# Relative attention on one core: each head's scores from its own 32 rows of the array, two heads into two banks, and the causal mask of the turned scores made by a select on GpSimd

## The reference

```python
xn = _layernorm(x, axis=-1)
Qh, Kh, Vh = heads of xn @ W_q + b_q, xn @ W_k + b_k, xn @ W_v + b_v
idx = clip(k - q, -2, 2) + 2
scores = einsum('bhqd,bhkd->bhqk', Qh, Kh)
scores = (scores + einsum('bhqd,qkd->bhqk', Qh, rel_k_table[idx])) / scale
scores = where(causal, scores, -1e9)
attn = softmax(scores)
out = einsum('bhqk,bhkd->bhqd', attn, Vh) + einsum('bhqk,qkd->bhqd', attn, rel_v_table[idx])
return out @ W_o + b_o
```

## Time and profile before

| | |
|---|---|
| median of 3 runs | 3927.83 us (3923.24 to 3929.47) |
| the profiled execution: its time, its span | 3928.65 us, 3926.6 us |
| mean granted TensorE clock over the span | 0.986 |
| relative attention, first to last instruction | from the start to about 564 us |
| one sequence (four groups) in it | 63.63 us |
| busy share of the span: TensorE, VectorE, ScalarE, GpSimd | 94%, 78%, 58%, 66% |

### The profile page before, as it was taken

One profiled execution on the slowest core, in us unless ns is written; L12 is line 12 of the kernel. 1 busy time (PEld: TensorE's weight loads), 2 busy tenths in 40 slices (PEclk: granted clock), 3 DMA queues, 4 the chain that ended last, 5 costly groups with the idle time before them and its releaser, 6 DMA issues.

```text
span 3926.6 us, 163773 instructions
## 1 busy us (share of the span) xinstructions
PE 3690.6 (94%) x67712; PEld 2844.7 (72%) x67712; DVE 3058.0 (78%) x5829; ACT 2270.7 (58%) x4270; POOL 2597.4 (66%) x3029
## 2 busy tenths in 40 slices
PE   5999979999999999999999999999999999999998
PEld 3555557777767777677877678787677876777876
DVE  7666658888778888788887788887788887888876
ACT  3555546666546666456666366665466664566653
POOL 4545538787547887367887288775477873687870
PEclk8999989999999999999999999999999999999999
DMA  1000002222212222122222122222122221222220
GB/s 44 4 6 4 6 28 68 56 60 60 58 32 59 59 57 59 41 49 60 61 57 56 30 65 57 59 61 58 32 60 58 59 56 41 54 57 58 60 52 22
DMA packets 136313, 189.08 MB, mean 48 GB/s; under 512 B 38006, under 2 KB 58484, under 8 KB 135412
## 3 DMA queue, kind: packets, MB, share of 16 engines
q1 hardware_dynamic: 135540, 178.23, 17.7%
HBM read 22.67 MB, written 2.10 MB: 6 GB/s over the span
## 4 chain that ended last, share of the span: by engine, by line
PE 76%; issue 4%; DVE 2%; POOL 2%; ACT 0%; DMA 0%; POOLq 0%; SPq 0%; DVEq 0%; ACTq 0%
PE PS L1270 18%; PE PS L1417 10%; PE PS L1256 10%; PE PS L1294 8%; PE PS L1280 8%; PE PS L1258 8%; PE PS L1257 8%; PE PS L1476 2%; PE PS L1411 2%; PE PS L1454 1%; PE PS L1447 1%; POOL t L1182 1%; PE PS L1442 1%; POOL t L1187 0%; DVE m L1800 0%
## 5 line engine op out<-in xcount | busy, mean ns | idle before, releaser
L1182 POOL TENSOR_TENSOR t<-t 128x1024 f32<-128x1024 f32 x384 | 908.0, 2370 | 363.9 <-DVE t L1762 362.6
L1187 POOL TENSOR_TENSOR t<-t,rn 128x1024 f32<-128x1024 f32 x384 | 723.6, 1905 | 29.8 <-POOL rn L150 27.3
L1542 ACT ACTIVATE va<-PS 128x512 f32<-128x512 f32 x384 | 229.8, 599 | 614.4 <-PE PS L1258 611.6
L1760 DVE TENSOR_TENSOR t<-PS,rope 128x512 f32<-128x512 f32 x768 | 523.2, 681 | 26.1 <-ACT sq L1577 24.5
L1256 PE MATMUL PS<-w_hi,xh 128*128 128x512 f32 x1152 | 514.2, 446 | 22.3 <-DVE xl L1063 11.3
L1577 ACT ACTIVATE sq<-PS 128x512 f32<-128x512 f32 x768 | 454.1, 593 | 33.0 <-PE PS L1258 17.7
L1270 PE MATMUL PS<-constants,t 128*128 128x128 f32 x3072 | 443.8, 277 | 19.8 <-POOL t L1187 12.8
L1258 PE MATMUL PS<-w_lo,xh 128*128 128x512 f32 x1152 | 458.5, 398 | 0.0
L1257 PE MATMUL PS<-w_hi,xl 128*128 128x512 f32 x1152 | 457.5, 397 | 0.0
L1767 DVE TENSOR_REDUCE ss<-sq 128x16 f32<-128x1024 f32 x384 | 448.3, 1209 | 0.0
L1270 PEld LDWEIGHTS PS<-constants,t 128*128 128x128 f32 x3072 | 351.9, 141 | 68.9 <-POOL t L1187 15.9
(11 more groups left out here) (168 smaller groups left out, 7869.8 us busy)
## 6 DMA issues: line engine op xcount, KB each, us to landing
vs<-va SPq DMA_DIRECT2D x768, 130.0 KB
vs<-va SPq DMA_DIRECT2D x768, 65.0 KB
t<-in_L_ffn_Wqkv SPq DMA_DIRECT2D x18, 512.0 KB, 4.4
w_out<-in_L_ffn_Wo SPq DMA_DIRECT2D x6, 512.0 KB, 3.9
a_normed<-in_L_attn_x SPq DMA_DIRECT2D x8, 256.0 KB, 7.0
a_xo<-in_L_attn_x SPq DMA_DIRECT2D x8, 256.0 KB, 2.8
out<-total SPq DMA_DIRECT2D x8, 256.0 KB, 3.5
w_raw<-in_L_ffn_W SPq DMA_DIRECT2D x6, 341.0 KB
```

The lines of the kernel that those rows point to most:

```text
L1182: pool.tensor_tensor(mine[:, i, :], mine[:, i, :], t2[:, i, :], ALU.add).then_inc(done, 1)
L1187: pool.tensor_tensor(h, h, bc(rn[:, H * i:H * (i + 1)], 2, HB), ALU.mult).then_inc(done, 1)
L1760: dve.tensor_tensor(o1, src, bc(rope[:, 2 * i, t, :], 1, 8), ALU.mult)
```

## The change

Four things change, all in `relative_attention`.

- `kT` has one tensor per group in place of four: no zeros, no copies. `join_keys` is one instruction on 128 rows, where it was four of 32 rows. The zero fill at the start goes.
- A score product takes only the 32 rows of its head. The two heads of a piece follow one another directly, on different rows of the array and into different banks.
- The last piece (j = 4), which held four heads in 256 columns each, becomes two pieces of two heads (j = 4 and 5), each 256 columns in each of two banks. `PIECES` is 6.
- The turned scores have no mask ahead of them. Instead, `close_future` on GpSimd writes zero over the future keys in `probs` after the exponentials, one select for each piece. `values` waits for it (`opened`) and no longer for ScalarE. `values(y, 0)` moves behind j = 3, and `values(y, 2)` behind the first turned piece of the next group. `weights` waits for the values of the group before piece by piece.

```diff
-        PIECES = 5
+        PIECES = 6
-        JOINS = 1 + G
+        JOINS = 2
-        kT = sb("a_kT", [P, NG, G, N], F32R)
+        kT = sb("a_kT", [P, NG, N], F32R)
...
             def join_keys(y):
                 wait_used(pool, ("proj", y, 1))
-                for r in range(G):
-                    rows = slice(32 * r, 32 * (r + 1))
-                    pool.wait_ge(joined, JOINS * y + 1 + r)
-                    pool.tensor_tensor(kT[rows, y % NG, r, 1:N], high[rows, 1, 0:N - 1].bitcast(F32), lowT[rows, 1, 0:N - 1],
-                                       ALU.add).then_inc(joined, 1)
-                pool.wait_ge(joined, JOINS * (y + 1))
+                pool.tensor_tensor(kT[:, y % NG, 1:N], high[:, 1, 0:N - 1].bitcast(F32), lowT[:, 1, 0:N - 1],
+                                   ALU.add).then_inc(joined, 1)
+
+            def close_future(y, j):
+                wait_used(pool, ("turn", y, j))
+                at, n = ((0, 1), (4 * P, 2), (8 * P, 1))[j // 2]
+                now = heads_of(j, at, n * P).rearrange("p g (n c) -> p g n c", n=n)
+                pool.affine_select(now, now, [[0, 2], [0, n], [1, P]], ALU.is_gt, 0.0, base=0, channel_multiplier=-1).then_inc(opened, 1)
...
             for y in range(GROUPS):
                 s, p = divmod(y, NG)
+                for j in range(3):
+                    close_future(y, j)
+                if y + 3 < GROUPS:
+                    join_queries(y + 3)
+                for j in range(3, PIECES):
+                    close_future(y, j)
...
-                q = lambda t: qT[:, g, P * t:P * (t + 1)]
-                k = lambda r, n: kT[:, g, r, 0:P * n]
+                blocks = (((3, 0, 4),), ((2, 0, 3), (0, 3, 1)), ((1, 0, 2),))[j // 2]
                 for a in range(2):
...
+                    at, n = ((3, 1), (2, 2), (1, 1))[j // 2]
+                    shut(tiles_of(bank(me, a), at, n), far_mask)
+                for t, at, n in blocks:
+                    for a in range(2):
+                        rows = head(j, a)
+                        done = score(bank(me, a)[:, P * at:P * (at + n)], qT[rows, g, P * t:P * (t + 1)], kT[rows, g, 0:P * n])
...
+                for t, at in (((0, 0),), ((3, 0), (1, 1)), ((2, 0),))[j // 2]:
+                    for a in range(2):
+                        rows = head(j, a)
+                        done = pe.matmul(bank(me, a)[:, P * at:P * (at - t) + N], kT[rows, g, P * t:P * (t + 1)],
+                                         qm[rows, y % 2, P * t:N], start=True, stop=True, skip_group_check=True)
...
-                for j in ((0, 1), (2, 3), (4,), ())[kt]:
-                    wait_used(pe, ("turn", y, j))
+                pe.wait_ge(opened, PIECES * y + (2, 4, 6, 4)[kt])
...
-                if y and j == 0:
-                    act.wait_ge(val_mm, 4 * y)
+                if y:
+                    act.wait_ge(val_mm, 4 * (y - 1) + (1, 3, 4)[j // 2])
...
-            dve.memset(kT[:].rearrange("p n g c -> p (n g c)").bitcast(F32), 0.0).then_inc(filled_in, 1)
             norm(0, TPS, 0)
```

More of the change, by code:

```diff
@@ L52 @@
 C_FAR = C_MQ0 + 2 * W
-C_FART = C_FAR + P
-C_SEL = C_FART + P
+C_SEL = C_FAR + P
 C_NEAR = C_SEL + P
@@ L365, in per_tile_head, with heads_of @@
             return h.rearrange("p t (h d) -> p t h d", h=H)
-        def of_heads(b, n):
-            return b[:, 0:G * n].rearrange("p (g c) -> p g c", g=G)
+        def heads_of(j, at, n):
+            return probs[:, 2 * (j % 2):2 * (j % 2) + 2, at:at + n]
         @block.sync
@@ L538, in turned @@
                 wait_slot(pe, me)
-                k = lambda r, t: kT[:, g, r, P * t:P * (t + 1)]
-                q = lambda t: qm[:, y % 2, P * t:N]
-                for a in range(2):
-                    b, r = bank(me, a), 2 * (j % 2) + a
-                    if j < 2:
-                        shut(b[:, 0:P], far_mask_t)
-                        done = score(b[:, 0:4 * P], k(r, 0), q(0))
-                    elif j < 4:
-                        shut(tiles_of(b, 0, 2), far_mask_t)
-                        score(b[:, 0:P], k(r, 3), q(3))
-                        done = score(b[:, P:4 * P], k(r, 1), q(1))
-                    else:
-                        shut(every_second(b, 0), far_mask_t)
-                        for h in range(2):
-                            done = score(b[:, 2 * P * h:2 * P * (h + 1)], k(2 * a + h, 2), q(2))
+                for t, at in (((0, 0),), ((3, 0), (1, 1)), ((2, 0),))[j // 2]:
[3 more added lines that the diff above has]
+                                         qm[rows, y % 2, P * t:N], start=True, stop=True, skip_group_check=True)
                 done.then_inc(filled(me), 1)
@@ L629, in _ @@
                     turned(y, j)
+                    if j == 0 and y:
+                        values(y - 1, 2)
                     if j == 0 and p == 1 and s + 1 < B:
@@ L637, in _ @@
                             turn_sums(s - 1, 3)
+                    if j == 3:
                         values(y, 0)
@@ L652, in _ @@
                 values(y, 3)
-                values(y, 2)
+            values(GROUPS - 1, 2)
             for i in range(TPS):
@@ L756, in maximum @@
                 else:
-                    target, source = maxima[:, y % 2, :, 5], bank(me).rearrange("p a (h c) -> p (a h) c", h=2)
+                    target, source = pair[:, :, 5], bank(me)[:, :, 0:2 * P]
                 dve.tensor_reduce(target, source, X, ALU.max).then_inc(used(me), 1)
@@ L841, in _ @@
             dve.wait_ge(const_in, 16)
+            dve.tensor_copy(kT[:, :, 0], rank["const"][:, C_SHUT:C_SHUT + 1].broadcast_to([P, NG])).then_inc(filled_in, 1)
             dve.wait_ge(filled_in, 2)
-            for r in range(G):
-                rows = slice(32 * r, 32 * (r + 1))
-                dve.tensor_copy(kT[rows, :, r, 0], rank["const"][rows, C_SHUT:C_SHUT + 1].broadcast_to([32, NG])).then_inc(filled_in, 1)
-            dve.wait_ge(filled_in, 2 + G)
             dve.wait_ge(bias_made, 10)
```

37 lines of the change are left out of this document (9 added, 28 removed).

## The result

| | before | after |
|---|---|---|
| median of the runs | 3925.53 us (4 runs, 3922.84 to 3929.47) | 3993.78 us (4 runs, 3984.91 to 3995.63) |
| the profiled execution's span | 3926.6 us | 3993.4 us |
| last copy of the sums begins | 551.42 us | 602.74 us |
| span behind it, the windowed layers above all | 3375.2 us | 3390.7 us |
| mean granted clock | 0.986 | 0.955 |

The ratio is 1.0164 (1.0152 to 1.0177): **slower by 1.6%**, where 3867 us and "faster" were predicted. The stage is 51 us longer, not 62 us shorter (54 and 8), and the windowed layers, which keep every instruction, take 15.5 us more.

What follows compares the result with a forecast made beforehand. TensorE's stream was taken to bound the relative attention stage. The sum was 3928.65 - 54 (groups) - 8 (start) + 1 (end) = 3867.7, given as 3867 us because the profiled execution is 0.8 above the median; range 3836 to 3905.

Steps and rivals of the forecast that it cites:

- 54 and 8: Relative attention: 54 us saved by 1.7 us net in each of 32 groups, 8 us by the earlier start.
- Prices of the pieces: TensorE's score pieces: 0.89 us for j = 0, 1; 1.11 for j = 2, 3; 0.67 for j = 4, 5.
- Rival 1: TensorE's score pieces: weight loads or shape changes cost the gain, 3905 or 3887 us; chance 0.24, including no overlap.
- Selects: GpSimd's selects over future keys: 3.5 us per group, bounds 2.8 and 5.1, so its load is no matter.
- the 1.5 us at which cover would be gone: GpSimd: at 1.5 us per select, the work covering both moved value products' waits for selects would no longer suffice.
- rival 3: Slow selects make GpSimd bound the relative attention stage: 4017 us at 7 ns per element; chance 0.07.
- Start: Start of the kernel: 5 us gained without the zero fill, 3 more from fewer key joins beside VectorE's norm.
- At granted clock 1.00: Relative attention stage: TensorE's clock read as 1.00 in the earlier profile, with prices and sum built on it.
- The last sentence of the prediction: Signs against it: select over 1.5 us, pairs 0.2 us apart, or stage clock leaving 1.00 because of 32-row strips.
- 0.3 us per group: Part of TensorE's 2.0 us saving per group lost to growing waits on VectorE's maxima, leaving 1.7 us net.
- the 3.8 us "that are there": TensorE's existing waits for VectorE's maxima per sequence, 1.29 us direct and 2.5 in held-back loads, expected to grow.
- The layers "unchanged": Windowed layers behind relative attention: every instruction is kept, so their time was counted unchanged.

Runs made afterwards that it cites:

- e4: Kernel before the change with one line moved: VectorE's zero fill of the keys behind the first norm instead of ahead of it; ratio to before 1.0009.
- e13: Kernel of e9 with four more 512-column mask products ahead of the second and third turned piece of each first group; ratio to before 1.0154.
- e5: Kernel before with selects for turned masks and moved value products; five pieces, all rows, zero fill behind the first norm; ratio to before 1.0023.
- e1: Changed kernel with score products on all 128 rows again (four padded key tensors, four joins, fill behind the norm); ratio to before 1.0045.
- e2: As e1, but natural score products on 32-row strips and only the turned ones on all rows; ratio to before 1.0154.
- e3: Changed kernel with 64-row strips in place of 32, two key tensors holding two heads each; ratio to before 1.0053.
- e12: Kernel before with GpSimd's near products moved into the fourth group and VectorE's sums over them behind the fourth maxima; ratio to before 1.0047.
- e9: Changed kernel with six 512-column mask products laid into TensorE's wait for the turned queries in every fourth group; ratio to before 1.0118.
- e7: Changed kernel with the masks on turned scores put back as products on all 128 rows, selects kept; ratio to before 1.0333.
- e15: Changed kernel with the previous group's last value products set ahead of the first turned piece instead of behind it; ratio to before 1.0224.
- e10: Changed kernel with GpSimd's near products moved into the fourth group and VectorE's sums over them behind the fourth maxima; ratio to before 1.0147.
- e14: Kernel of e5 with VectorE's zero fill of the keys ahead of the first norm, as in the kernel before; ratio to before 1.0028.

## Why the prediction was wrong

- **Prices of the pieces: right.** 0.88 for 0.89 us, 1.08 for 1.11, 0.68 and 0.63 for 0.67; no load or change of shape cost more. Rival 1 was not it.
- **Selects: right,** 2.97 us per group between the bounds, and rival 3 has no part. No select comes near the 1.5 us at which cover would be gone.
- **Start: near in the sum,** 9.5 us earlier for 8. How the fill (5) and the joins (3) share it isn't shown: e4, which only moves the fill, gains 3.1 us at the same place.
- **"At granted clock 1.00": this step failed, and it is the largest error.** The sum took the clock of the earlier trace rows for granted. The last sentence of the prediction named this way to fall, but it had neither a chance nor a price there; the 0.07 for "slower" was all for slow selects. In the changed kernel the third and fourth stretch ran at 0.61 and 0.68. At 1.00 the third stretch is 13.2 us (e13) and the fourth 18.05 less the filler's eight products of 0.21 us, thus 16.3, so a sequence would be 13.85 + 18.82 + 13.2 + 16.3 = 62.2 us (an estimate put together from two kernels). It is 71.7: **9.5 us a sequence, some 76 us in eight**, is the clock.
- **"0.3 us per group" taken back: this term failed too.** By the same estimate a sequence at full clock gains 63.6 - 62.2 = 1.4 us, which is 0.4 per group and not 1.7. TensorE's busy time did fall, by 1.81 us in the first stretch and 1.11 in the second, but it went into waits. The prediction looked for them at the maxima and shared them evenly. They came at the near terms, at the queries and at the sums, which it had called TensorE's time to catch up. Its starting point was too high as well: the 3.8 us "that are there" add a wait of the weight loads (2.1 us) to the wait of the product behind it (1.29), which is the same one, and TensorE idles 63.63 - 60.88 = 2.75 us in all. Some 5.4 us a sequence, 43 us in eight.
- The two make 119 us; the last copy is at 602.7 where the prediction has 551.4 - 62 = 489, 113 us off. With the 15.5 us of the layers that is the whole miss of 127 us, within 2.
- **The layers "unchanged":** their instructions are, their time is not. 15.5 us more here, and from 3374 to 3407 us over the kernels, in part by the clock (e5) and in part by idle time.

That the strips bring the clock down here is shown, by e1 and e2. What the clock asks for can be told only in part. Strips lower it (e1, e2, e3). So do longer waits on full rows (e12, and one sequence before). Work laid into a wait brings part of it back (e9), and work laid elsewhere doesn't (e7). All of this fits one account: the changed kernel does its work in less of TensorE's time and array, and stretches with little of both are followed by the lower level, at which projections take 2.08 us for 1.02. e15 and the spread within e13 do not follow from it, so the account is supported, not settled. The Trainium skill's page "TensorE: Matmul & The Clock Gate", section "HAM oscillation — how this bites in real kernels", tells of a kernel whose waits for DMA make the clock swing between its levels; the stretches at 0.61 and 1.00 within one sequence agree with it in kind, while the waits here are for VectorE.

For VectorE's differences the Trainium skill has a rule: its page "SBUF — State Buffer", section "SBUF: two separate sides", has a VectorE instruction with two SBUF inputs and a GpSimd instruction that reads SBUF exclude one another, for the whole of whichever starts first. 2.41 us for two differences beside the near products, and 0.24 us for one on average without them (e10), agree.

## What to carry to other kernels

A cheaper form of the bounding engine's work is worth its price only if the engine's clock and its partners keep up: read the granted clock by stretch, and ask of each saved microsecond which wait it turns into. A change that makes TensorE do more in less time should carry a rival "the clock falls", priced from rows: here the stretches it touches cost 9.5 us more. Take compound changes apart: up to the last copy of the sums, selects in place of masks on full rows won 16 us, the sixth piece alone lost 9.5 (both with the fill behind the norm, which alone won 3.7 in e4), both together lost 5 (e1), and the strips, added last, lost 46; one measurement of them all shows none of it. None of the fifteen is faster than the old program, for even the best stage lost its gain behind it.

## What was not expected of the hardware

- Masks laid into a wait of 1.38 us made a program 0.5% faster than without them (ratios 1.0118 and 1.0164, 14.7 us of it in the stage); smaller masks in every turned piece made it 1.7% slower (1.0333).
- The same instructions took 63.9 us (clock 1.00) and 76.3 us (0.80) in two sequences of one execution (e13).
- Windowed layers with the same instructions took 3374 to 3407 us behind different stages. In e5 TensorE was busy 23.1 us longer over the same number of products; in e14 its idle time without a releaser in front of a single line was 14 us longer than before.
- Two operations of VectorE on 16 elements took 2.41 us beside GpSimd's products on 512, and 0.28 us in the best group of the same execution (from 354.18 us).
